# Four of the eight batches of x1 are read back during the expert tiles, and VectorE adds one and a half of them

## The chip, the core and the metric

The kernel runs on one core of a Trainium2 chip. The metric is the time on the device, in microseconds (us), of one execution; lower is better. Times in a trace are counted from the start of its span.

## The reference

The input x has 8 batches of 512 tokens with 256 features. Two blocks follow each other, each of the form x + layernorm(block(layernorm(x))):

```python
x = x + layernorm(s4d(layernorm(x)))      # x1: state-space convolution over 512 tokens (by FFT), skip, layernorm
x = x + layernorm(moe(layernorm(x)))      # 8 experts, each token goes to its best 2
# moe: z = layernorm(x); w = softmax weights of the top 2 experts, scaled to sum 1
#      x + sum over experts of w[e] * (gelu(z @ W1[e] + b1[e]) @ W2[e] + b2[e])
```

What matters here is the last line: the output is x1 plus the normalised result of the second block. The kernel calls the first block's result x1 and the second block's result, summed over a token's two experts, y.

## The kernel before, in words

All of it is one program in which each engine runs its own list of instructions, ordered by hand, and waits on semaphores. SyncE (`sp`) issues all plain DMA transfers, on one queue, in the order of its list. GpSimd (`pool`) issues the indirect ones.

First comes the s4d block, one batch at a time. Each batch of x1 (128 partitions x 4 x 256 numbers, 512 KB) is stored to a DRAM buffer `x1_dram`, and the normalised rows are scattered by expert into `z_rows`. Then come the tiles: 71 (`TILES`) tiles of 128 rows, each of one expert. The first 14 (`FIRST`) are taken while the last batch is still being routed; from tile 14 on the remaining tiles run through the experts in order, so that the first expert is through at the latest with tile 14 + 32 - 1. For a tile SyncE reads its rows (`load_z`, two buffers), PE transposes them, does the first layer (`first_layer`, L1487), transposes the hidden rows and does the second layer (`second_layer`, L1511, which counts up `l2_mm`). ScalarE weighs the result and GpSimd scatters it, adding, into `y_rows`. `load_z(t)` waits until tile t-2 has been transposed, and `release(t)` lets GpSimd's scatters go on. The weights of all eight experts stay in SBUF for the whole time (`ws`, 16 KB of each partition for one expert, from offset 0). In tiles 20, 21 and 22 SyncE also reads the batches 7, 6 and 5 of x1 back into `x1m` (L446).

When the last scatter has landed, the tail begins. The eight batches are taken from the last to the first; n counts them (n = 0 is batch 7). SyncE reads y of each into `yr`, over the place of the weights (L459). Ahead of n = 2 it reads batch 4 of x1 (L456), ahead of n = 6 the batches 0 to 3 in one transfer (L458). For each n VectorE takes mean and variance (`spread_of`, L1224 and L1227), ScalarE the root (`root`, L706), VectorE the factors (`scale`, L1235 to L1237), ScalarE writes the normalised batch into `acc` in four instructions (`close`, L711; `m_fin` counts finished batches, and the last one in two halves), GpSimd adds x1 in place (`add`, L1331, counts `m_out`), and SyncE stores it (L463). Of the last batch GpSimd adds the first half and VectorE the second (L1248, `m_last`). VectorE's list runs two batches ahead: `scale(n)` comes before `spread_of(n + 2)`, and a wait in the one holds the next.

Of the kernel before, what the change touches and what calls it, by code (L numbers as in the profile page):

```python
# [17 lines left out]
F32 = mybir.dt.float32  # L18
# [7 lines left out]
P = 128  # L26
B, T, H, N = 8, 512, 256, 64
# [11 lines left out]
HEAD = 5  # L39
FIRST = -(-(HEAD * T - (E - 1) * (P - 1)) // P)  # L40
ROWS = E * REGION
ROUND = 12582912.0
TURN = 6.283185
W = H + 3
TRASH = B * T
KB = 1024
# [20 lines left out]
def program(nc, x, fwd_tab, inv_tab, lag_tab, swap_in, phase_in, ident_in, upper_in, tile_tab, lar, aim, cre, cim,  # L67
            ldt, d_skip, ln_w, ln_b, ffn_g, ffn_b, r_w, r_b, w1, b1, w2, b2, out, dbg=None):
    sems = {}

    def sem(name):
        if name not in sems:
            sems[name] = nc.alloc_semaphore(name)
        return sems[name]

    def at(name, shape, dt, off):
        return nc.alloc_sbuf_tensor_at(name, shape, dt, offset=BASE + off)
# [88 lines left out]
    x1m = at("x1m", [P, B, 4, H], F32, 112 * KB + 64)  # L166
# [23 lines left out]
    cmp_t = at("cmp_t", [P, TILES + 1 - FIRST, E], F32, o0 + 64)  # L190
    tf = at("tf", [P, 3, TILES + 1], F32, o0 + 2560)
    iot = at("iot", [P, 3, TILES + 1], F32, o0 + 12544)
    yr = at("yr", [P, B, 4, H], F32, 0)
    acc = at("acc", [P, B, 4, H], F32, 64 * KB)
    psum = nc.alloc_psum_tensor("psum", [P, 8 * 512], F32)

# [41 lines left out]

    z_rows = nc.dram_tensor("z_rows", [ROWS, W], F32, kind="Internal").ap()
    y_rows = nc.dram_tensor("y_rows", [B * T + 2 * P, H], F32, kind="Internal").ap()  # L240
    x1_dram = nc.dram_tensor("x1_dram", [P, B, 4, H], F32, kind="Internal").ap()
# [13 lines left out]
    def gate(eng):  # L255

        eng.sem_inc(sem("gate"), 1)
# [30 lines left out]
    def buf(b):  # L288

        return (0, 1, 2, 3, 0, 1, 4, 5)[b]  # L290

    def sent(b):

        return 128 * (1 + (b in (4, 5)))
# [19 lines left out]
    def slot_of(b):  # L314

        return (0, 1, 2, 3, 7, 6, 5, 4)[b]

    with nc.Block() as block:

        @block.sync  # L320
        def _(sp):
# [61 lines left out]
            def load_z(t):  # L383

                if t in (0, FIRST):
                    sp.wait_ge(sem("tab_ready"), 1 + (t == FIRST))
                row = sp.value_load(tab[0:1, 0, t:t + 1], min_val=0, max_val=ROWS - P)
                if t >= 2:
# [11 lines left out]
            def pad(e):  # L400

                behind = sp.value_load(padi[0:1, e:e + 1], min_val=0, max_val=ROWS - P)
                sp.dma_start(z_rows[bass.ds(behind, P), :], zpad[:, :]).then_inc(sem("pads"), 16)
# [36 lines left out]
            for t in range(FIRST, TILES):  # L440
                load_z(t)
                release(t - 6)
                if 20 <= t < 23:

                    b = B - 1 - (t - 20)
                    sp.dma_start(x1m[:, slot_of(b)], x1_dram[:, b]).then_inc(sem("x1_in"), 16)  # L446
            for t in range(TILES - 6, TILES):
                release(t)

# [3 lines left out]
            sp.wait_ge(sem("y_out1"), 16 * (TILES // 2))  # L453
            for n in range(B):
                if n == 2:
                    sp.dma_start(x1m[:, slot_of(4)], x1_dram[:, 4]).then_inc(sem("x1_in"), 16)  # L456
                if n == 6:
                    sp.dma_start(x1m[:, 0:4], x1_dram[:, 0:4]).then_inc(sem("x1_in"), 16)  # L458
                sp.dma_start(yr[:, n], y_tok[:, B - 1 - n]).then_inc(sem(f"y_in{n}"), 16)  # L459
            for n in range(B):  # L460
                sp.wait_ge(sem("m_out"), n + 1)
                ks = slice(0, 2 if n == B - 1 else 4)
                sp.dma_start(out[:, B - 1 - n, ks], acc[:, n, ks]).then_inc(sem("stored"), 16)  # L463
            sp.wait_ge(sem("m_last"), 1)
            sp.dma_start(out[:, 0, 2:4], acc[:, B - 1, 2:4]).then_inc(sem("stored"), 16)
            sp.wait_ge(sem("stored"), 16 * (B + 1))

        @block.scalar
        def _(act):
# [254 lines left out]
        def _(dve):  # L724
            seq = Seq(dve, sem("dve_seq"))
            V = nc.vector
# [48 lines left out]
            V.memset(one_half[:, :], 0.5)  # L775
            V.memset(rnd[:, :], ROUND).then_inc(sem("one"), 1)
            seq.inc(V.memset(carry_b[:, :], 0.0))
# [22 lines left out]
            do(V.tensor_scalar(ang[:, 3], theta, T / 2.0, None, ALU.mult))  # L800
            do(V.tensor_scalar(sm[:, 10:14], ang[:, :, :, :], ROUND, ROUND, ALU.add, ALU.subtract))
            V.tensor_tensor(ang[:, :, :, :], ang[:, :, :, :], sm[:, 10:14], ALU.subtract).then_inc(sem("k_ang"), 1)
# [439 lines left out]
            for n in range(B):  # L1242
                scale(n)
                if n + 2 < B:
                    spread_of(n + 2)
            dve.wait_ge(sem("m_fin"), B + 1)
            dve.wait_ge(sem("x1_in"), 80)
            V.tensor_tensor(acc[:, B - 1, 2:4], acc[:, B - 1, 2:4], x1m[:, 0, 2:4], ALU.add).then_inc(sem("m_last"), 1)  # L1248

        @block.gpsimd  # L1250
        def _(pool):
            G = nc.gpsimd
            def combine(row, u):
                n, par = row.b * 2 + u, row.par
                pool.wait_ge(sem("mult_done"), n + 1)
                ks = slice(2 * u, 2 * u + 2)
                G.tensor_tensor(yf[par][:, 0, ks], yf[par][:, 0, ks], tmp[u][:, 0],  # L1257
                                ALU.subtract).then_inc(sem("yf_ready"), 1)
                G.tensor_tensor(yf[par][:, 1, ks], yf[par][:, 1, ks], tmp[u][:, 1],  # L1259
                                ALU.add).then_inc(sem("yf_ready"), 1)  # L1260

            def fold(b):

                pool.wait_ge(sem("xn_ready"), b + 1)
                G.tensor_tensor(pm[b][:, 0], xn[b % 3][:, 0:2], xn[b % 3][:, 2:4], ALU.add).then_inc(sem("pm_ready"), 1)  # L1265
                G.tensor_tensor(pm[b][:, 1], xn[b % 3][:, 0:2], xn[b % 3][:, 2:4], ALU.subtract).then_inc(sem("pm_ready"), 1)

            def scatter(row, lo, hi):

                pool.wait_ge(sem("pos_ready"), row.b + 1)  # L1270
                for i in range(lo, hi):
                    pool.indirect_dma_start(z_rows, bass.IndirectOffsetOnAxis(ap=pos[row.par][:, i // 4, i % 4:i % 4 + 1], axis=0),  # L1272
                                            zn[buf(row.b)][:, i % 4], None).then_inc(sem(f"scattered{buf(row.b)}"), 16)

            def step(n):
                nxt, cur, tail, last_tail = (Row(n, k) for k in (1, 0, -2, -LAG))

                last = Row(n, -LAG - 1)
                if cur.live and cur.b:
                    if cur.b > 1:  # L1280
                        pool.wait_ge(sem("x1_mean"), cur.b - 1)
                    combine(cur, 1)
                if last.live and n <= B:
                    scatter(last, 3, 8)
                if nxt.live:
                    if nxt.b > 1:
                        pool.wait_ge(sem("o_ready"), nxt.b - 1)
                    combine(nxt, 0)
                    if nxt.b == 0:
                        combine(nxt, 1)  # L1290
                if last_tail.live and n < B:
                    scatter(last_tail, 0, 3)
                elif n == B:
                    scatter(last_tail, 0, 8)
                    scatter(tail, 0, 8)
                for b in FOLDS.get(n, ()):
                    fold(b)

            for b in range(4):
                fold(b)  # L1300
            for n in range(-1, B + 1):
                step(n)


            def scatter_y(t):

                q = t % 2
                if t:
                    pool.wait_ge(sem("released"), t)
                    gate(pool)  # L1310
                if t >= 2:
                    pool.wait_ge(sem(f"y_out{q}"), (t - q) * 8)
                    gate(pool)
                pool.wait_ge(sem("yw_ready"), t + 1)
                gate(pool)
                pool.indirect_dma_start(y_rows, bass.IndirectOffsetOnAxis(ap=dst[t % 8][:, 0:1], axis=0),  # L1316
                                        yw[t % 6][:, :], None, compute_op=ALU.add).then_inc(sem(f"y_out{q}"), 16)

            for b in range(2, B):
                pool.wait_ge(sem(f"zn_stored{buf(b)}"), sent(b) // 8)  # L1320
            pool.wait_ge(sem("trash_set"), 32)
            for t in range(TILES):
                if t == EARLY:
                    scatter(Row(B - 1, 0), 0, 8)
                scatter_y(t)

            def add(n, ks):
                pool.wait_ge(sem("m_fin"), n + 1)
                if n in (0, 3):
                    pool.wait_ge(sem("x1_in"), 80 if n else 48)  # L1330
                G.tensor_tensor(acc[:, n, ks], acc[:, n, ks], x1m[:, slot_of(B - 1 - n), ks], ALU.add).then_inc(sem("m_out"), 1)  # L1331

            for n in range(B):
                add(n, slice(0, 2 if n == B - 1 else 4))

        @block.tensor
        def _(pe):
# [300 lines left out]
```

## Time and profile before

| | |
|---|---|
| median of 3 runs | 563.23 us (562.65 to 569.51) |
| profiled execution, its own time | 566.21 us |
| its span | 564.4 us |
| mean granted clock of TensorE | 0.913 |
| busy: PE, VectorE, ScalarE, GpSimd | 81%, 79%, 67%, 47% of the span |

The trace is of one execution, whose own time is the span with 1.8 us around it. The tail from the first read of y (530.94 us) to the end of the span is 33.5 us, in which PE does nothing.

### The profile page before, as it was taken

How to read it: one execution, taken by the hardware profiler on the slowest of the kernel's cores; microseconds unless marked ns; L12 is line 12 of the kernel's file. 1: busy time of each engine (PE TensorE's matmuls, PEld its weight loads, DVE VectorE, ACT ScalarE, POOL GpSimd, SP SyncE). 2: the span in 40 equal slices, each digit the busy share in tenths (PEclk: the TensorE clock that was granted, in tenths of full speed). 3: DMA queues.
4: the chain of work that ended last, by engine and by line, in shares of the span. 5: the costliest groups of instructions: out<-in, count | busy, mean ns of one | idle time of the engine just before them, and what ended most of it. 6: DMA issues, size and time to landing. Idle time of an engine off the chain costs nothing.

```text
span 564.4 us, 11667 instructions
## 1 busy us (share of the span) xinstructions
PE 455.0 (81%) x2730; PEld 393.6 (70%) x2730; DVE 443.1 (79%) x1492; ACT 377.3 (67%) x928; POOL 267.3 (47%) x195
## 2 busy tenths in 40 slices
PE   0296899978999988468868999999999999999100
PEld 0136888857988876247757888999999999998100
DVE  6999785999898987765766878877888878887282
ACT  6991864455666656767634777777777777776184
POOL 0000349544566877365175344445444444445365
PEclk9997989988999996687986999999999999999655
DMA  6303730042224466496145458444555545444696
GB/s 166 135 1 121 285 117 1 0 130 77 104 94 153 152 213 208 137 326 219 30 133 94 80 93 189 77 77 77 78 79 82 80 82 77 77 72 54 145 400 273
DMA packets 47615, 70.35 MB, mean 125 GB/s; under 512 B 7616, under 2 KB 37184, under 8 KB 47040
## 3 DMA queue, kind: packets, MB, share of 16 engines
q1 hardware_dynamic: 34256, 51.82, 27.6%
q0 software_dynamic: 13296, 17.80, 19.1%
q8 instruction: 26, 0.43, 0.3%
q14 instruction: 37, 0.30, 0.2%
HBM read 37.90 MB, written 31.70 MB: 123 GB/s over the span
## 4 chain that ended last, share of the span: by engine, by line
PE 51%; DVE 24%; ACT 10%; issue 5%; DMA 4%; POOL 2%; another core or an unknown queue 1%; SPq 1%; DVEq 1%; POOLq 0%; ACTq 0%
PE psum L1487 16%; PE psum L1511 15%; PE psum L1497 5%; PE psum L1407 4%; DVE ws L934 2%; PE psum L1471 2%; DMA yr<-y_rows 2%; DVE st L739 2%; PE psum L1378 2%; PE psum L1365 2%; PE psum L1427 2%; ACT xn L492 1%; DMA y_rows<-yw,dst 1%; ACT dump L652 1%; ACT ws L589 1%
## 5 line engine op out<-in xcount | busy, mean ns | idle before, releaser
L1316 POOL DMA_INDIRECT y_rows<-yw,dst x71 | 113.1, 1593 | 142.1 <-SPq L398 76.6
L1487 PE MATMUL psum<-ws,z_hl 128*128 x426 | 120.7, 420 | 9.3 <-DVE ws L934 6.4
L1511 PE MATMUL psum<-ws,h_hl 128*128 x852 | 118.3, 289 | 0.6 <-DVE h_hl L1100 0.6
L1511 PEld LDWEIGHTS psum<-ws,h_hl 128*128 128x128 f32 x852 | 105.8, 192 | 0.8 <-issue 0.8
L1487 PEld LDWEIGHTS psum<-ws,z_hl 128*128 128x128 f32 x426 | 77.3, 195 | 24.4 <-issue 11.2
L1272 POOL DMA_INDIRECT z_rows<-zn,pos x64 | 70.2, 1097 | 28.8 <-issue 17.1
L634 ACT ACTIVATE hg<-hb 128x512 f32<-128x512 f32 x71 | 44.9, 633 | 33.8 <-DVE hb L1094 32.0
L597 ACT ACTIVATE z_f<-psum,gb 128x128 f32<-128x128 f32 x142 | 57.2, 453 | 10.5 <-issue 4.5
L1407 PE MATMUL psum<-yf,it 128*128 128x256 f32 x256 | 62.0, 400 | 2.6 <-DVE r L1121 2.6
L1378 PE MATMUL psum<-pm,ft 128*128 128x256 f32 x256 | 59.9, 390 | 0.4 <-DVE tmp L920 0.2
L627 ACT CAST h_hl<-psum 128x512 fp32r<-128x512 f32 x71 | 41.5, 585 | 25.7 <-PE psum L1497 21.4
L1407 PEld LDWEIGHTS psum<-yf,it 128*128 128x128 f32 x256 | 50.9, 202 | 10.6 <-POOL yf L1259 3.2
L1081 DVE CAST z_hl<-z_f 128x256 fp32r<-128x256 f32 x71 | 21.0, 295 | 43.6 <-PE psum L1487 35.1
L1378 PEld LDWEIGHTS psum<-pm,ft 128*128 128x128 f32 x256 | 48.9, 195 | 7.7 <-issue 1.1
L1094 DVE TENSOR_TENSOR hb<-psum,b1r 128x512 f32<-128x512 f32 x71 | 48.5, 684 | 5.5 <-remote 3.1
L1100 DVE TENSOR_TENSOR h_hl<-psum,h_hl 128x512 fp32r<-128x512 f32 x71 | 48.3, 680 | 2.3 <-ACT h_hl L627 2.0
L1497 PE MATMUL psum<-ident,hg 128*128 128x128 f32 x284 | 43.5, 276 | 1.6 <-ACT hg L634 1.4
L1497 PEld LDWEIGHTS psum<-ident,hg 128*128 128x128 f32 x284 | 35.9, 142 | 12.3 <-ACT hg L634 2.5
L1257 POOL TENSOR_TENSOR yf<-yf,tmp 128x512 f32<-128x512 f32 x16 | 24.4, 1523 | 39.4 <-DVE o L1147 29.7
L1265 POOL TENSOR_TENSOR pm<-xn 128x512 f32<-128x512 f32 x8 | 10.2, 1280 | 68.8 <-ACT xn L492 68.8
L607 ACT ACTIVATE yw<-y_sb,wt 128x256 f32<-128x256 f32 x71 | 35.7, 503 | 4.5 <-DVE y_sb L1111 3.2
L1083 DVE TENSOR_TENSOR z_hl<-z_f,z_hl 128x256 fp32r<-128x256 f32 x71 | 30.2, 426 | 2.4
(222 smaller groups left out, 843.3 us busy)
## 6 DMA issues: line engine op xcount, KB each, us to landing
z_in<-z_rows SPq DMA_DIRECT2D x71, 129.5 KB
w_raw<-in_dram SPq DMA_DIRECT2D x16, 512.0 KB, 5.9
xs<-in_dram SPq DMA_DIRECT2D x8, 512.0 KB, 5.4
x_dram<-xs SPq DMA_DIRECT2D x8, 512.0 KB
y_rows<-zn SPq DMA_DIRECT2D x8, 512.0 KB, 3.3
yr<-y_rows SPq DMA_DIRECT2D x8, 512.0 KB, 7.2
out_dram<-acc SPq DMA_DIRECT2D x7, 512.0 KB, 5.1
b1r<-in_dram SPq DMA_DIRECT2D x8, 256.0 KB
```

Source lines behind the costliest of these rows:

```text
L597: last = nc.scalar.activation(z_f[:, k], ps_z[:, k], ACT.Identity, bias=gb[:, 1, k:k + 1], scale=gb[:, 0, k:k + 1])
L627: nc.scalar.copy(h_hl[t % 2][:, 0], ps_t).then_inc(sem("h_high"), 1)
L634: nc.scalar.activation(hg[t % 2][:, :], hb[:, :], ACT.Gelu).then_inc(sem("hg_ready"), 1)
L1094: V.tensor_tensor(hb[:, :], ps_h[t % 2], b1r[:, bass.ds(e, 1)].rearrange("p a f -> p (a f)"), ALU.add).then_inc(sem("hb_ready"), 1)
L1100: V.tensor_tensor(h_hl[t % 2][:, 1], ps_t, h_hl[t % 2][:, 0].bitcast(F32), ALU.subtract).then_inc(sem("h_split"), 1)
L1272: pool.indirect_dma_start(z_rows, bass.IndirectOffsetOnAxis(ap=pos[row.par][:, i // 4, i % 4:i % 4 + 1], axis=0), zn[buf(row.b)][:, i % 4] ...
L1316: pool.indirect_dma_start(y_rows, bass.IndirectOffsetOnAxis(ap=dst[t % 8][:, 0:1], axis=0), yw[t % 6][:, :], None, compute_op=ALU.add).the ...
L1378: last = TE.matmul(fw[u][c][:, k], ft[:, c, t, kt * P:(kt + 1) * P], pm[row.b][:, c, t], start=t == 0, stop=t == 1)
L1407: last = TE.matmul(iv[c][:, j * H:(j + 1) * H], it[:, c, k, j * P:(j + 1) * P], yf[row.par][:, c, k], start=k == 0, stop=k == KT - 1)
L1487: last = TE.matmul(ps_h[q], z_hl[q][:, a, k], w_at(e, c, k * F, F), start=n == 0, stop=n == 5)
L1497: last = TE.transpose(ps_t[:, k], hg[t % 2][:, k * P:(k + 1) * P], ident[:, :])
L1511: last = TE.matmul(ps_y[q], h_hl[q][:, a, k], w_at(e, c, 1024 + k * H, H), start=n == 0, stop=n == 11)
```

## The change

Four batches of x1 (0 to 3) get a buffer of their own, `x1a`, at offset 0, the place of the first expert's weights; `yr` moves 16 KB further on. SyncE reads them one by one after the reads of z for the tiles 56, 58, 60 and 62, behind a wait for 46 finished second layers. The 2 MB read ahead of n = 6 goes. Batch 4 keeps its place ahead of n = 2 and has its own semaphore. GpSimd's first add now waits for all seven batches that are read during the tiles. GpSimd adds the batches n = 0 to 5 and the first half of n = 6; VectorE adds the second half of n = 6 and both halves of n = 7. The stores of the last two batches are four halves, in the order in which the list expects them.

```diff
+LATE = (56, 58, 60, 62)
...
-    yr = at("yr", [P, B, 4, H], F32, 0)
+    yr = at("yr", [P, B, 4, H], F32, 16 * KB)
+    x1a = at("x1a", [P, 4, 4, H], F32, 0)
...
+    def x1_of(b):
+
+        return x1a[:, b] if b < 4 else x1m[:, slot_of(b)]
...
+                if t in LATE:
+
+                    sp.wait_ge(sem("l2_mm"), FIRST + B * T // P)
+                    b = 3 - LATE.index(t)
+                    sp.dma_start(x1a[:, b], x1_dram[:, b]).then_inc(sem("x1_in"), 16)
...
                 if n == 2:
-                    sp.dma_start(x1m[:, slot_of(4)], x1_dram[:, 4]).then_inc(sem("x1_in"), 16)
-                if n == 6:
-                    sp.dma_start(x1m[:, 0:4], x1_dram[:, 0:4]).then_inc(sem("x1_in"), 16)
+                    sp.dma_start(x1m[:, slot_of(4)], x1_dram[:, 4]).then_inc(sem("x1_four"), 16)
                 sp.dma_start(yr[:, n], y_tok[:, B - 1 - n]).then_inc(sem(f"y_in{n}"), 16)
-            for n in range(B):
+
+            def store(n, lo, hi):
+
+                sp.dma_start(out[:, B - 1 - n, lo:hi], acc[:, n, lo:hi]).then_inc(sem("stored"), 16)
+
+            for n in range(B - 2):
                 sp.wait_ge(sem("m_out"), n + 1)
-                ks = slice(0, 2 if n == B - 1 else 4)
-                sp.dma_start(out[:, B - 1 - n, ks], acc[:, n, ks]).then_inc(sem("stored"), 16)
+                store(n, 0, 4)
+            sp.wait_ge(sem("m_half"), 1)
+            store(B - 2, 2, 4)
             sp.wait_ge(sem("m_last"), 1)
-            sp.dma_start(out[:, 0, 2:4], acc[:, B - 1, 2:4]).then_inc(sem("stored"), 16)
-            sp.wait_ge(sem("stored"), 16 * (B + 1))
+            store(B - 1, 0, 2)
+            sp.wait_ge(sem("m_out"), B - 1)
+            store(B - 2, 0, 2)
+            sp.wait_ge(sem("m_last"), 2)
+            store(B - 1, 2, 4)
+            sp.wait_ge(sem("stored"), 16 * (B + 2))
...
-            dve.wait_ge(sem("m_fin"), B + 1)
-            dve.wait_ge(sem("x1_in"), 80)
-            V.tensor_tensor(acc[:, B - 1, 2:4], acc[:, B - 1, 2:4], x1m[:, 0, 2:4], ALU.add).then_inc(sem("m_last"), 1)
+            dve.wait_ge(sem("x1_in"), 112)
+            dve.wait_ge(sem("m_fin"), B - 1)
+            V.tensor_tensor(acc[:, B - 2, 2:4], acc[:, B - 2, 2:4], x1_of(1)[:, 2:4], ALU.add).then_inc(sem("m_half"), 1)
+            for u in range(2):
+                dve.wait_ge(sem("m_fin"), B + u)
+                ks = slice(2 * u, 2 * u + 2)
+                V.tensor_tensor(acc[:, B - 1, ks], acc[:, B - 1, ks], x1_of(0)[:, ks], ALU.add).then_inc(sem("m_last"), 1)
...
             def add(n, ks):
                 pool.wait_ge(sem("m_fin"), n + 1)
-                if n in (0, 3):
-                    pool.wait_ge(sem("x1_in"), 80 if n else 48)
-                G.tensor_tensor(acc[:, n, ks], acc[:, n, ks], x1m[:, slot_of(B - 1 - n), ks], ALU.add).then_inc(sem("m_out"), 1)
-
-            for n in range(B):
-                add(n, slice(0, 2 if n == B - 1 else 4))
+                if n == 0:
+                    pool.wait_ge(sem("x1_in"), 112)
+                if n == 3:
+                    pool.wait_ge(sem("x1_four"), 16)
+                G.tensor_tensor(acc[:, n, ks], acc[:, n, ks], x1_of(B - 1 - n)[:, ks], ALU.add).then_inc(sem("m_out"), 1)
+
+
+            for n in range(B - 1):
+                add(n, slice(0, 2 if n == B - 2 else 4))
```

## Rows read from the trace of the kernel before

**Rows 1.** The head of the page.
```profile
span 564.4 us, 11667 instructions
```

**Rows 2.** The chain of waits in the tail: start us, us, what.
```profile
534.88 13.45 DMA yr<-y_rows
```

**Rows 3.** Stretches: us, busy and instructions of each engine, clock, DMA share, GB/s.
```profile
535.00:541.00 6.00, 0.00 (x0) 0.00 (x0) 5.76 (x31) 3.00 (x8) 0.31 (x1) 0.50 1.02 416
```

**Rows 4.** VectorE's timeline: start us, us, what, idle before and releaser.
```profile
547.15 0.16 DVE L1237 TENSOR_TENSOR rm<-xb,psum 128x4 f32<-128x4 f32 x1
548.35 1.40 DVE L1224 BATCH_NORM_STATS2 st<-yr 128x6 f32<-128x256 f32 x4 [1.04 <-DMA yr<-y_rows]
...
556.95 1.07 DVE L1248 TENSOR_TENSOR acc<-acc,x1m 128x512 f32<-128x512 f32 x1 [3.45 <-ACT acc L711]
```

**Rows 5.** ScalarE's timeline in the tail.
```profile
538.53 2.07 ACT L711 ACTIVATE acc<-yr,rm 128x256 f32<-128x256 f32 x4 [0.20 <-DVE rm L1237]
...
547.35 2.08 ACT L711 ACTIVATE acc<-yr,rm 128x256 f32<-128x256 f32 x4
...
550.67 2.07 ACT L711 ACTIVATE acc<-yr,rm 128x256 f32<-128x256 f32 x4 [0.20 <-DVE rm L1237]
...
552.88 4.04 ACT L711 ACTIVATE acc<-yr,rm 128x256 f32<-128x256 f32 x8
```

**Rows 6.** GpSimd's timeline in short windows; a row with x2 holds two instructions.
```profile
540.69 2.35 POOL L1331 TENSOR_TENSOR acc<-acc,x1m 128x1024 f32<-128x1024 f32 x1 [11.98 <-ACT acc L711]
...
547.59 4.67 POOL L1331 TENSOR_TENSOR acc<-acc,x1m 128x1024 f32<-128x1024 f32 x2
...
552.82 2.35 POOL L1331 TENSOR_TENSOR acc<-acc,x1m 128x1024 f32<-128x1024 f32 x1 [0.56 <-ACT acc L711]
...
555.12 4.02 POOL L1331 TENSOR_TENSOR acc<-acc,x1m 128x1024 f32<-128x1024 f32 x2
...
557.43 1.71 POOL L1331 TENSOR_TENSOR acc<-acc,x1m 128x512 f32<-128x512 f32 x1
```

**Rows 7.** SyncE's timeline, the last three stores.
```profile
557.50 0.33 SPq L463 DMA_DIRECT2D out_dram<-acc  x1
559.17 0.33 SPq L463 DMA_DIRECT2D out_dram<-acc  x1
559.54 0.43 SPq L465 DMA_DIRECT2D out_dram<-acc  x1
```

**Rows 8.** SyncE's waits from 526 us on: us in total, times, longest.
```profile
SPq L318 <- DMA out_dram<-acc: 2.4, 1, 2.4
SPq L318 <- PEq L318: 1.8, 1, 1.8
```

**Rows 9.** The timeline of tiles 20 to 22, SyncE's reads of x1.
```profile
338.04 0.33 SPq L446 DMA_DIRECT2D x1m<-x_dram  x1
...
340.26 0.33 SPq L446 DMA_DIRECT2D x1m<-x_dram  x1
...
342.95 0.33 SPq L446 DMA_DIRECT2D x1m<-x_dram  x1
```

**Rows 10.** The chain of waits in the same tiles.
```profile
337.39 1.40 PE psum L1487 x6
...
340.84 1.41 PE psum L1487 x6
...
344.30 0.45 issue
344.74 1.66 PE psum L1487 x6
...
348.45 1.41 PE psum L1487 x6
```

**Rows 11.** Stretches with the third of those reads, and of quiet tiles (columns as in group 3).
```profile
341.00:344.50 3.50, 3.30 (x24) 2.78 (x22) 2.85 (x10) 2.75 (x8) 1.56 (x1) 1.00 1.04 253
...
440.00:460.00 20.00, 20.00 (x140) 18.18 (x140) 16.50 (x53) 15.83 (x41) 10.01 (x7) 1.00 0.51 81
```

## The prediction

> **What bounds the kernel now.** I read the page first, then the chain of waits, then each engine's timeline of the last 35 us, and last the stretch of the tiles in which the kernel already reads x1. The span is 564.4 us [rows 1]. The change touches two stretches: the tiles, where the order of the work is PE's, and the tail after the last tile. Nothing before the reads of tile 56 changes, and y's new place, 16 KB further on, moves no instruction.
>
> In the tail the chain of waits shows one long piece: the seventh read of y, issued at 534.88, lands 13.45 us later, at 548.33 [rows 2]. It stands behind the read of four batches of x1 (2 MB). In that stretch the DMA engines are full, at 416 GB/s [rows 3]. VectorE has finished its small work on the batch before at 547.31 and sits idle for 1.04 us until that read lands [rows 4]. ScalarE's scaling of the sixth batch inherits it: the first five follow each other at (547.35 - 538.53) / 4 = 2.20 us, the sixth comes 3.32 us after the fifth [rows 5], so 1.12 us late. GpSimd, which adds x1, is the slower engine (2.35 us a batch; 2.30 from start to start): it keeps busy through five batches and could start the sixth at 547.59 + 2 x 2.30 = 552.2, but idles 0.56 us and starts it at 552.82 [rows 6]. From then on GpSimd sets the end: two whole batches and half of the last, finished at 557.43 + 1.71 = 559.14. SyncE then issues two stores, at 559.17 and 559.54 [rows 7]; the last one is waited for 2.4 us and 1.8 us of closing waits follow [rows 8]. From the start of the last store to the end of the span: 564.4 - 559.54 = 4.86 us.
>
> **The change, part by part.**
>
> Reads leave the tail. Four batches are 2.1 MB; at 416 GB/s that is 5.0 us less in front of the seventh and eighth y. The seventh then lands near 548.33 - 5.0 = 543.3, 4 us before VectorE wants it at 547.31. The 1.04 us idle goes. ScalarE's sixth batch starts at 547.35 + 2.20 = 549.55 and ends at 551.6. The seventh and eighth shift by the same 1.12 us: the seventh ends at 552.88 + 2.07 - 1.12 = 553.83, the eighth's first half at 554.82, its second at 556.92 - 1.12 = 555.80. What is late next is GpSimd: its sixth add starts when the fifth is done, 552.2 instead of 552.82. This step alone is worth 0.6 us, not 1.1.
>
> Half of batch seven and the first half of batch eight go from GpSimd to VectorE. GpSimd then ends its sixth add at 552.2 + 2.35 = 554.55 and has half a batch left; VectorE has three halves, ready at 553.83, 554.82 and 555.80. What they cost beside each other is read from the one place where both add. VectorE's half ran from 556.95 to 558.02 [rows 4]. GpSimd's whole add had begun at 555.12 and ended at 555.12 + 2.35 = 557.47, and its half ran from 557.43 to 559.14 [rows 6]. So VectorE's ended 0.55 us after GpSimd's whole add, and GpSimd's half 1.12 us after VectorE's; half of 2.35 is 1.18. That looks like taking turns: each instruction spends its overlap waiting and then needs 0.55 (VectorE) or 1.12 (GpSimd). I count in turn: from 554.55, three halves of 0.55 and one of 1.12 make 2.8, so everything is added at 557.3 to 557.4, whichever engine goes first. Before, the same count after GpSimd's sixth add (555.17) was 2.30 + 0.55 + 1.12 = 3.97. The gain of this step is 1.2 us.
>
> If instead the two only slow each other, the durations 1.07 and 1.71 stand for themselves: VectorE 553.85 + 3 x 1.07 = 557.06, GpSimd 554.5 + 1.71 = 556.2, done at 557.1. With no interference at all VectorE's last half would end at 555.80 + 0.55 = 556.4 and GpSimd's at 555.7. These are the good end; the bad end is the turns, with a start that slips.
> The Trainium skill (SBUF — State Buffer, Who interferes with whom) says that a VectorE instruction with both inputs in SBUF contends with a GpSimd instruction that reads SBUF, and that one of them blocks for the other's whole instruction. By that rule the end of the adds is the 557.4 of the turns, and without it the 557.1 of the plain durations; it speaks against moving the adds to VectorE, and the two durations above fit it.
>
> Stores. The last two are reordered into four halves. If VectorE ends last, SyncE has already issued the third and the last starts at about 557.45; if GpSimd ends last, two stores follow each other as before (0.37 us apart) and the last starts at about 557.8. I take 557.6, against 559.54: 1.9 us earlier. In the 2 us before it 1 MB of stores is under way, the same as before (one whole batch and two halves), so I keep the 4.86 us behind it. Were the stores closer together than that, 0.26 MB at 416 GB/s would add 0.6 us.
>
> Four reads enter the tiles. SyncE issues each in 0.33 us behind a tile's read of z [rows 9]. The new wait in front of them asks for 46 finished second layers. Behind it in SyncE's queue stand the next reads of z (PE waits for them) and the releases of GpSimd's scatters. It costs nothing: the read of z for tile 56, just ahead, has waited for the transposes of tile 54, which PE issues after the second layer of tile 50. The reads' own cost has one precedent, the three reads at tiles 20 to 22, one a tile. PE's chain shows one disturbance there: 0.45 us of "issue" and a first layer of 1.66 instead of 1.41 us [rows 10], 0.70 us in all, behind the third read, where the DMA share stood at 1.04 against 0.51 in a quiet stretch [rows 11]. The first two reads cost nothing. The new reads come every second tile, 6.9 us apart. One read of 0.52 MB takes 1.26 us of all engines, so the share over two tiles rises to about 0.51 + 1.26 / 6.9 = 0.69, and no pile like that of the third read should form. Bounds: 0 and 4 x 0.70 / 3 = 0.93 us; between them no row decides, and I take the middle, 0.45. GpSimd's first add waits for all seven reads in the tiles; the last is issued near 342.95 + 40 x 3.45 = 481, almost 60 us ahead of that add. The fifth batch keeps its place in the tail, third in the queue, and the fourth add that waits for it comes at 547.59.
>
> **Sum.** -0.6 (stall) - 1.2 (adds) - 0.1 (stores) + 0.45 (tiles) = -1.4 us. The profiled execution took 566.21 us (564.4 of it the span) and would take 564.8. That run stands 3.0 us above the median of the runs, 563.23, so I forecast 561.8. Nothing under 2% (11 us) can be told from no change here, and this change cannot reach it.
>
> **The rivals.**
> The adds run side by side: the last store starts between 556.5 and 557.15, 2.4 to 3.0 us early; less 0.45, the time is 560.7 to 561.3. For it: a good part of VectorE's 1.07 us might be sharing. Against it: the ends 0.55 and 1.12 us after each other.
> Slower: each late read stalls PE once. The place is the first layer after a read, the price the 0.70 us of the third read, so 2.8 us, and 563.23 - 1.9 + 2.8 = 564.1. It decides as soon as one read costs over 0.48 us. For it: z of the next tile is queued behind half a megabyte on the same queue. Against it: two of the three reads known cost nothing, and they came at twice the rate.
> The reads go and the end stays with the stores: four half stores and the whole one pile up and the last lands 0.6 us later, or the adds slip; half the gain is lost, 562.7 or so.
> A larger effect, a lower clock or long stalls of PE in the last tiles, has no row for it.
>
> **How the numbers follow.** The forecast has 0.50 (its own range 561.0 to 562.6), side by side 0.20, the lost gain 0.15, the stalling reads 0.12, something larger 0.03. The runs shown spread from 562.65 upward, so half a microsecond goes on either side: from 560.0, below the best of side by side, to 564.6, above the stalling reads. Faster by over 2%: 0.01; within: 0.97; slower: 0.02.
>
> **What would show it.** VectorE's seventh statistics follow at once, with no wait on a read of y. GpSimd has six whole adds in one row without idle time, and a half. The three VectorE adds and that half do not finish before 557.3 if they take turns, counted from the first add at 540.69. Tiles 56 to 63 keep the 3.45 us each of the tiles before (340.84 - 337.39 [rows 10]) but for one stall. Wrong it would be if PE shows a gap behind each read, if a VectorE half took 0.55 us beside a GpSimd add, or if the last store were waited for clearly over 2.4 us.

## The result and the profile after

The change made the kernel faster, by a little more than I forecast: 560.53 us median against 563.4 us, a difference of 2.9 us. The ratio of the means is 0.9936 with a 95% interval of 0.9910 to 0.9962, that is 3.6 us (2.1 to 5.1). I had forecast 561.8, a gain of 1.4 us, and had written that nothing under 2% can be told from no change here; the interval does tell it. The time lies inside the range and the direction is right; the size of the gain is not.

The head of the page of the kernel after, against [rows 1]; the profiled execution took 560.84 us:

```profile
span 558.8 us, 11672 instructions
```

The first read of y starts anywhere from 526.5 to 530.9 us in the traces of this study, so I count the tail from its own marks. From the first read of y to the end of the span it took 564.4 - 530.94 = 33.46 us before and 558.8 - 528.11 = 30.69 us after: 2.77 us less.

SyncE's timeline after, the reads of the tail and the last store, against [rows 7] (start us, us, what):

```profile
528.11 0.81 SPq L468 DMA_DIRECT2D yr<-y_rows  x2
528.96 0.43 SPq L467 DMA_DIRECT2D x1m<-x_dram  x1
529.43 2.96 SPq L468 DMA_DIRECT2D yr<-y_rows  x6
...
554.95 0.46 SPq L472 DMA_DIRECT2D out_dram<-acc  x1
```

VectorE's timeline after, against [rows 4]: the seventh statistics, at 544.51, follow the factors before them with no wait on a read. The only wait on y left is that for the first one.

```profile
531.78 1.41 DVE L1243 BATCH_NORM_STATS2 st<-yr 128x6 f32<-128x256 f32 x4 [9.24 <-DMA yr<-y_rows]
...
544.43 0.16 DVE L1256 TENSOR_TENSOR rm<-xb,psum 128x4 f32<-128x4 f32 x1
544.51 1.41 DVE L1243 BATCH_NORM_STATS2 st<-yr 128x6 f32<-128x256 f32 x4
...
551.21 1.19 DVE L1267 TENSOR_TENSOR acc<-acc,x1a 128x512 f32<-128x512 f32 x1 [1.55 <-ACT acc L730]
552.32 1.75 DVE L1271 TENSOR_TENSOR acc<-acc,x1a 128x512 f32<-128x512 f32 x1
...
553.99 0.68 DVE L1271 TENSOR_TENSOR acc<-acc,x1a 128x512 f32<-128x512 f32 x1
```

ScalarE's timeline after, against [rows 5]: the sixth batch follows the fifth 2.21 us later, where it was 3.32.

```profile
544.62 2.08 ACT L730 ACTIVATE acc<-yr,rm 128x256 f32<-128x256 f32 x4
...
546.83 2.08 ACT L730 ACTIVATE acc<-yr,rm 128x256 f32<-128x256 f32 x4
...
549.03 4.04 ACT L730 ACTIVATE acc<-yr,rm 128x256 f32<-128x256 f32 x8
```

GpSimd's timeline after, in short windows as in [rows 6]: the first row has the first four adds, then come the sixth and the half behind it. No row after the first has idle time in front of it.

```profile
537.96 9.28 POOL L1356 TENSOR_TENSOR acc<-acc,x1m 128x1024 f32<-128x1024 f32 x4 [12.20 <-ACT acc L730]
...
549.47 2.38 POOL L1356 TENSOR_TENSOR acc<-acc,x1a 128x1024 f32<-128x1024 f32 x1
...
551.77 1.75 POOL L1356 TENSOR_TENSOR acc<-acc,x1a 128x512 f32<-128x512 f32 x1
```

SyncE's waits in the tail after, against [rows 8]: the last store lands 2.1 us after its issue and 1.0 us of closing waits follow, where it was 2.4 and 1.8.

```profile
SPq L324 <- DMA out_dram<-acc: 2.1, 1, 2.1
...
SPq L324 <- PEq L324: 1.0, 1, 1.0
```

Here is the surprise. From the first GpSimd add, the last add of all ends at 554.67 - 537.96 = 16.71 us, as forecast (557.35 - 540.69 = 16.7), and the last store starts at 16.99 instead of 18.85, 1.86 us earlier, as forecast too (1.9). But behind it only 558.8 - 554.95 = 3.85 us follow, not the 4.86 that I kept. That is 1.0 us of gain that I had not counted, more than half of the 1.4 us that I forecast.

The chain of waits in the late tiles has one gap in PE, against [rows 10]: 0.15 us of issue and 0.25 us in the first layer, 0.40 us in all. I had put 0.45 there.

```profile
482.92 1.41 PE psum L1513 x6
...
486.38 0.15 issue
486.53 1.66 PE psum L1513 x6
...
490.24 1.41 PE psum L1513 x6
```

### The profile page after: what moved, and what is told of

It is laid out like the page before. It is cut to its first block, busy times and chain, and to the rows that moved or that the text cites. A ratio compares the mean times of both kernels' runs of the same rounds, so it can differ in the third digit from the quotient of the medians.

```text
span 558.8 us, 11672 instructions
## 1 busy us (share of the span) xinstructions
PE 450.2 (81%) x2730; PEld 388.9 (70%) x2730; DVE 445.0 (80%) x1494; ACT 376.2 (67%) x928; POOL 263.4 (47%) x194
## 4 chain that ended last, share of the span: by engine, by line
PE 48%; DVE 26%; ACT 14%; issue 6%; DMA 2%; POOL 1%; DVEq 1%; SPq 1%; another core or an unknown queue 0%; ACTq 0%; POOLq 0%
PE psum L1513 17%; PE psum L1537 15%; PE psum L1523 5%; PE psum L1497 3%; DVE ws L953 3%; ACT acc L730 2%; PE psum L1433 2%; DVE st L758 2%; PE psum L1391 2%; ACT dump L671 2%; DVE o L1166 1%; ACT ws L608 1%; PE psum L1404 1%; PE psum L1453 1%; DVE vq L885 1%
## 5 line engine op out<-in xcount | busy, mean ns | idle before, releaser
L1339 POOL DMA_INDIRECT y_rows<-yw,dst x71 | 111.2, 1566 | 144.4 <-SPq L404 84.1
L1404 PE MATMUL psum<-pm,ft 128*128 128x256 f32 x256 | 58.2, 382 | 0.4 <-DVE tmp L939 0.4
L1497 PE MATMUL psum<-ident,z_in 128*128 128x128 f32 x142 | 27.5, 276 | 7.2 <-issue 4.1
```

The lines of the kernel that those rows point to most:

```text
L1404: last = TE.matmul(fw[u][c][:, k], ft[:, c, t, kt * P:(kt + 1) * P], pm[row.b][:, c, t], start=t == 0, stop=t == 1)
L1497: last = TE.transpose(ps_z[:, k], z_in[q][:, k * P:(k + 1) * P], ident[:, :])
```

## The experiments

Two questions: why fewer microseconds follow the last store, and whether the terms of the sum are each of the size I gave them. The theories on the first were three: A, the closing varies from one execution to the next; B, it belongs to the kernel and hangs on the last store and the order of the stores; and C, which came out of the first four runs, it hangs on GpSimd.

**Both kernels again**, unchanged.

> The kernel before, unchanged, to see what one execution differs from the next. Ratio 1.00 by every theory. Theory A (the closing after the last store varies from one execution to the next, and the first trace of before had a long one): from the start of the last store to the end of the span comes out other than 4.86 us, at 3.8 to 4.9. Theory B (the closing belongs to the kernel: its last two stores follow 0.37 us apart): 4.86 us again, to 0.2 us. Both: from the first GpSimd add to the last store 18.85 us again, to 0.1 us, and at most one stall of PE after tile 23.

Ratio 1.0009 (0.9986 to 1.0032). The last store starts 18.86 us after the first add, and 4.83 us follow. The two traces of this kernel agree, so A has nothing left for it.

> The kernel after, unchanged. Theory A: the closing after the last store varies and may come out up to 4.9 us; theory B: 3.85 us again, to 0.2 us. Both: from the first GpSimd add to the last store 17.0 us. The tiles: if the late reads stall PE, one or more gaps of 0.4 to 0.7 us between tiles 56 and 66 again; if the one gap seen was chance, none or somewhere else. Ratio 0.993 to 0.996.

Ratio 0.9931 (0.9904 to 0.9959). The last store starts 556.22 - 539.25 = 16.97 us after the first add, and 3.88 us follow. PE has one gap in the late tiles, 0.66 us, this time right behind the third read.

**The reads alone.** The adds and stores of the kernel before, put into the kernel after:

```diff
...
-            dve.wait_ge(sem("m_fin"), B - 1)
-            V.tensor_tensor(acc[:, B - 2, 2:4], acc[:, B - 2, 2:4], x1_of(1)[:, 2:4], ALU.add).then_inc(sem("m_half"), 1)
...
+            dve.wait_ge(sem("m_fin"), B + 1)
+            V.tensor_tensor(acc[:, B - 1, 2:4], acc[:, B - 1, 2:4], x1_of(0)[:, 2:4], ALU.add).then_inc(sem("m_last"), 1)
...
-            for n in range(B - 1):
-                add(n, slice(0, 2 if n == B - 2 else 4))
+            for n in range(B):
+                add(n, slice(0, 2 if n == B - 1 else 4))
```

> The late reads and the tail without the 2 MB read, but the adds and stores of the kernel before. By my sum: GpSimd adds without idle, the last store 18.85 - 0.63 = 18.2 us after the first add. Theory A: closing between 3.8 and 4.9 us; theory B: 4.8 us, as before. Tiles 0 to 0.9 us longer. Ratio 0.999 to 1.000. A rival, that the reads alone bring most of the gain, would give 17.0 to 17.5 us and a ratio of 0.995.

Ratio 0.9990 (0.9963 to 1.0017). The 1.04 us wait for the seventh y is gone, but in this execution the second and third y came a little late, VectorE waited 0.30 and 0.27 us, and GpSimd idled 0.21 us. The last store starts 18.50 us after the first add, where 18.2 was expected, and 4.89 us follow. The gain is small, as expected, and not the bulk of the whole.

**The adds alone.** The reads of the kernel before (2 MB ahead of the seventh y), the adds and stores of the one after:

```diff
-LATE = (56, 58, 60, 62)
...
+                if n == 6:
+                    sp.dma_start(x1m[:, 0:4], x1_dram[:, 0:4]).then_inc(sem("x1_in"), 16)
...
```

> The reads of the kernel before, the adds and stores of the one after. By turns, with GpSimd's stall of 0.63 us kept and ScalarE's last batches 1.12 us late: 17.2 to 17.3 us from the first add to the last add, last store 17.3 us after the first add. Theory A: closing between 3.8 and 4.9 us; theory B: 3.85 us, as in the kernel after. No gap in PE beyond what the kernel before has. Ratio 0.995 to 0.998.

Ratio 0.9981 (0.9957 to 1.0004). The last add ends 17.35 us after the first one, where turns gave 17.2 to 17.3. The tail is 560.9 - 529.64 = 31.26 us, 2.2 us shorter than before; the runs show 0.0019 of 563.9, 1.1 us (-0.2 to 2.4). The last store starts at 557.11, 17.62 us after the first add, 0.3 us later than expected, and 3.8 us follow: the closing that B had forecast. So these four runs leave B standing.

Laid side by side, though, the four runs and the first two traces had one constant that was in neither theory: the span ends 5.21 to 5.30 us after the end of GpSimd's last add, whatever VectorE and the stores do. The next run was made to decide between B and this.

**GpSimd last of all**, in one execution.

```diff
                 add(n, slice(0, 2 if n == B - 2 else 4))
+            pool.wait_ge(sem("m_last"), 2)
+            G.memset(flag[:, :], 0.0)
```

> The kernel after, and behind its last add GpSimd waits for VectorE's last add and writes 128 numbers that nobody reads. Times from the first GpSimd add (kernel after: GpSimd's last add ends at 15.56, the last store starts at 16.99, the span ends at 20.84). Theory C (the span ends about 5.25 us after GpSimd's last instruction, which was so in all six traces, 5.21 to 5.30): GpSimd's last instruction ends at 16.85, the span at 22.1. Theory B (the end hangs on the last store, and the closing behind it on the order of the stores): 20.8, unchanged, since no store waits for the new instruction.

The span ends 559.6 - 537.49 = 22.11 us after the first add, 1.27 us later than in the kernel after, though no store waits for the new instruction and the last store starts where it did (16.98). GpSimd's timeline in that kernel:

```profile
537.49 9.27 POOL L1356 TENSOR_TENSOR acc<-acc,x1m 128x1024 f32<-128x1024 f32 x4 [11.99 <-ACT acc L730]
...
554.26 0.10 POOL L1362 MEMSET flag<- 128x1 f32 x1 [1.21 <-DVE acc L1271]
```

SyncE's waits there: the last store lands after 2.1 us as before, and the closing wait behind it grows from 1.0 to 2.3 us. The wait is put down to PE's queue, which had nothing to do for 30 us; the engine that was late is GpSimd.

```profile
SPq L324 <- PEq L324: 2.3, 1, 2.3
SPq L324 <- DMA out_dram<-acc: 2.1, 1, 2.1
```

**No contest for SBUF.** ScalarE writes the halves that VectorE adds into PSUM:

```diff
...
+    fin = {(B - 2, 1): bank(6), (B - 1, 0): bank(7), (B - 1, 1): bank(3)}
...
-                    last = nc.scalar.activation(acc[:, n, k], yr[:, n, k], ACT.Identity,
+                    last = nc.scalar.activation(closed(n, k // 2)[:, k % 2], yr[:, n, k], ACT.Identity,
...
-                V.tensor_tensor(acc[:, B - 1, ks], acc[:, B - 1, ks], x1_of(0)[:, ks], ALU.add).then_inc(sem("m_last"), 1)
+                V.tensor_tensor(acc[:, B - 1, ks], closed(B - 1, u), x1_of(0)[:, ks], ALU.add).then_inc(sem("m_last"), 1)
```

> The kernel after, but ScalarE puts the halves that VectorE adds into PSUM, so that VectorE's three adds have one input in SBUF. By turns (an add with two SBUF inputs and a GpSimd add take turns): no waiting any more, VectorE's halves take about 0.68 us each, the last ends at 15.8 us after the first GpSimd add instead of 16.71, GpSimd's half takes 1.2 us instead of 1.75 and ends at 15.0. If the two slow each other in another way, 1.07 to 1.2 us a half again and 16.7. End of the span: by theory C 15.0 + 5.25 = 20.2; by theory B 15.9 + 3.85 = 19.7. Ratio to before 0.992.

Ratio 0.9969 (0.9948 to 0.9989). VectorE's timeline in this kernel:

```profile
550.49 0.69 DVE L1274 TENSOR_TENSOR acc<-psum,x1a 128x512 f32<-128x512 f32 x1 [1.52 <-ACT psum L737]
551.41 0.69 DVE L1278 TENSOR_TENSOR acc<-psum,x1a 128x512 f32<-128x512 f32 x1 [0.22 <-ACT psum L737]
552.39 0.69 DVE L1278 TENSOR_TENSOR acc<-psum,x1a 128x512 f32<-128x512 f32 x1 [0.29 <-ACT psum L737]
```

And GpSimd's, in a short window, its half batch:

```profile
551.11 1.27 POOL L1363 TENSOR_TENSOR acc<-acc,x1a 128x512 f32<-128x512 f32 x1
```

VectorE's first two halves take 0.69 us each beside GpSimd's adds, where they took 1.19 and 1.75; GpSimd's half takes 1.27 where it took 1.75. VectorE's last add ends at 553.08 - 537.28 = 15.80, as turns had it. The span ends at 20.32, 5.22 us after GpSimd's last add, as C had it (20.2), and not at 19.7 as B had it. The ratio is a miss: 0.992 was expected, and the runs show no gain over the kernel after (0.9931 to 0.9955 in three comparisons), though in its trace the span ends 0.5 us sooner after the first add. Why, I do not know; the intervals overlap.

**Six adds on GpSimd, two batches on VectorE**, both inputs in SBUF. The last two batches are then stored in three parts, the seventh whole and the eighth in halves:

```diff
...
-            V.tensor_tensor(acc[:, B - 2, 2:4], acc[:, B - 2, 2:4], x1_of(1)[:, 2:4], ALU.add).then_inc(sem("m_half"), 1)
+            V.tensor_tensor(acc[:, B - 2], acc[:, B - 2], x1_of(1), ALU.add).then_inc(sem("m_half"), 1)
...
-            for n in range(B - 1):
-                add(n, slice(0, 2 if n == B - 2 else 4))
+            for n in range(B - 2):
+                add(n, slice(0, 4))
```

> The kernel after, but GpSimd adds only six whole batches and VectorE all of the last two (both inputs in SBUF). GpSimd's last add ends 13.9 us after its first. VectorE: a whole batch from 13.9 to 15.0, the halves to 15.7 and 16.3; last store at 16.35. Theory C: 13.9 + 5.25 = 19.1, unless the last store with its 2.1 to 2.5 us of landing ends later, then 19.2 to 19.5. Theory B: 16.35 + 3.85 = 20.2. Ratio to before 0.990 to 0.992.

Ratio 0.9916 (0.9899 to 0.9933). The span ends 19.72 us after the first add, 1.1 us sooner than in the kernel after. GpSimd's last add ends at 550.65, 5.85 us before the end, more than the 5.2 to 5.3 of the others: it is no longer what the end waits for. SyncE's waits there: the store's landing comes last, and almost no closing wait is left.

```profile
SPq L324 <- DMA out_dram<-acc: 2.5, 1, 2.5
SPq L324 <- PEq L324: 0.2, 1, 0.2
```

**Both together**, six adds on GpSimd and two batches added from PSUM (the two edits above, with all four halves of the last two batches in PSUM).

> Both together: GpSimd adds six whole batches, VectorE two, from PSUM. VectorE's last add ends 15.8 us after GpSimd's first, the last store starts at 15.9 and lands by 18.5. Theory C: 13.9 + 5.25 = 19.1. Theory B: 15.9 + 3.85 = 19.7. Ratio to before 0.990, to the kernel after 0.997.

Ratio 0.9931 (0.9918 to 0.9945). The last add ends at 15.80 as expected, but the last store's issue is done at 16.76, no earlier than with six adds alone (16.83), its landing takes 2.7 us, and the span ends at 19.84, where C had 19.1 and B 19.7. GpSimd is out of the way here, so the two theories are not told apart by it. The 0.36 us of faster adds are lost between SyncE's issue and the landing; which of the two costs how much I did not separate. The ratio, expected at 0.990, is a miss too.

**The two best beside each other.**

> Six whole adds on GpSimd, VectorE the last two batches, beside the kernel after on the same chip. The trace of its first run ended 19.7 us after GpSimd's first add, 1.1 us sooner than the kernel after, and there the last store's landing ended last (2.5 us, then 0.2 us), not GpSimd (5.85 us before the end). Expected again: 19.6 to 19.8; ratio to before 0.990 to 0.993, about 0.002 under the kernel after in this call.

> The kernel after, beside the one above. Span end 20.8 us after GpSimd's first add and 5.2 to 5.3 us after GpSimd's last. If the gain in the runs is what the traces show (2.8 us in the tail, 0 to 0.7 us given back in the tiles), the ratio to before is 0.995 to 0.996; if the runs hold another gain that the traces do not show, 0.993 as twice before.

Six adds: ratio 0.9932 (0.9907 to 0.9957), end 19.90 us after the first add (6.01 after GpSimd's last). Kernel after: 0.9955 (0.9935 to 0.9975), end 20.80 (5.27 after GpSimd's last), one gap in PE of 0.44 us. The six-add version is clearly faster than the kernel before; over the kernel after it is 0.9 to 1.1 us ahead in the tails of the traces, while the intervals of the runs overlap.

**The late reads one a tile.**

```diff
-LATE = (56, 58, 60, 62)
+LATE = (56, 57, 58, 59)
```

> The kernel after with its four late reads after the tiles 56, 57, 58 and 59, one a tile as in tiles 20 to 22. If the stall of PE comes of reads piling up, one or two stalls of 0.3 to 0.7 us within four tiles of the third read. If it is chance (with reads two tiles apart four traces of seven had one stall, three had none), none or one, and anywhere from tile 56 on. Tail as in the kernel after: end 20.8 us after GpSimd's first add.

In this one execution the reads pile up, and further than expected: three tiles in a row come late. PE's timeline around the third read (467.26) and the fourth (469.29) shows one transpose that waits for its rows of z, and two first layers that start late. Three tiles take 477.91 - 466.05 = 11.86 us, 1.5 us more than 3 x 3.45. Only 0.19 us of it is put down to the landing of z; the late first layers stand as "issue", and what held them is not shown.

```profile
466.05 0.38 PE L1497 MATMUL psum<-ident,z_in 128*128 128x128 f32 x2
...
469.84 0.44 PE L1497 MATMUL psum<-ident,z_in 128*128 128x128 f32 x2 [0.19 <-DMA z_in<-z_rows]
470.69 1.66 PE L1513 MATMUL psum<-ws,z_hl 128*128 x6 [0.41 <-issue]
474.02 0.38 PE L1497 MATMUL psum<-ident,z_in 128*128 128x128 f32 x2
474.60 1.67 PE L1513 MATMUL psum<-ws,z_hl 128*128 x6 [0.19 <-issue]
477.91 0.38 PE L1497 MATMUL psum<-ident,z_in 128*128 128x128 f32 x2
```

The stretch from 470 to 474 us in that kernel, against [rows 11] (columns as there):

```profile
470.00:474.00 4.00, 3.59 (x24) 3.05 (x24) 2.69 (x8) 2.60 (x7) 0.00 (x0) 1.00 1.06 297
```

All marks in one table, in us from the start of GpSimd's first add, worked out from the timelines and spans ("issued" is the end of SyncE's issue; the spans are read to 0.1 us):

| kernel | GpSimd's last instruction ends | VectorE's last add ends | last store issued | span ends | end less GpSimd's last |
|---|---|---|---|---|---|
| before | 18.45 | 17.33 | 19.28 | 23.71 | 5.26 |
| before, again | 18.45 | 17.34 | 19.29 | 23.69 | 5.24 |
| reads alone | 18.10 | 16.97 | 18.93 | 23.39 | 5.29 |
| adds alone | 16.20 | 17.35 | 18.07 | 21.41 | 5.21 |
| after | 15.56 | 16.71 | 17.44 | 20.84 | 5.28 |
| after, again | 15.55 | 16.70 | 17.42 | 20.85 | 5.30 |
| after, third | 15.53 | 16.69 | 17.42 | 20.80 | 5.27 |
| GpSimd last of all | 16.87 | 16.71 | 17.44 | 22.11 | 5.24 |
| halves from PSUM | 15.10 | 15.80 | 16.90 | 20.32 | 5.22 |
| late reads one a tile | 15.56 | 16.71 | 17.44 | 20.79 | 5.23 |
| six adds | 13.87 | 16.16 | 16.83 | 19.72 | 5.85 |
| six adds, again | 13.89 | 16.18 | 16.85 | 19.90 | 6.01 |
| six adds, from PSUM | 13.86 | 15.80 | 16.76 | 19.84 | 5.98 |

In the first ten rows, those up to the late reads one a tile, the last column is 5.21 to 5.30, while the last store moves by 2.4 us. Only where GpSimd is done early does the landing of the stores take over.

The traces also show what the end waits for. The line that opens the block of engine programs (L324) holds each engine's closing instructions, among them a DRAIN (count, least/median/most ns, first and last start in us). In the kernel after:

```profile
L324 POOLq DRAIN  x1: 7406/7406/7406, 551.1 to 551.1; - x1
L324 DVEq DRAIN  x1: 1605/1605/1605, 553.1 to 553.1; - x1
L324 SPq DRAIN  x1: 7/7/7, 557.7 to 557.7; - x1
```

With GpSimd last of all:

```profile
L324 POOLq DRAIN  x1: 5132/5132/5132, 554.2 to 554.2; - x1
```

With six adds:

```profile
L324 POOLq DRAIN  x1: 7931/7931/7931, 547.8 to 547.8; - x1
...
L324 SPq DRAIN  x1: 7/7/7, 556.3 to 556.3; - x1
```

GpSimd's DRAIN ends at 558.5, 559.3 and 555.7, each time 5.0 us after its last instruction; VectorE's ends within 0.1 us of its last add. In the first two kernels GpSimd's DRAIN is the last of all, and the span ends 0.2 to 0.3 us behind it. With six adds SyncE's is the last, at 556.3.

## Why the prediction was wrong in its size

*The stall goes* (-0.6): right. VectorE's wait for the seventh y is gone, ScalarE's batches follow each other at 2.2 us to the end, GpSimd adds seven times without idle time.

*The adds, taken in turn* (-1.2): right, to 0.1 us. In the trace after, GpSimd's sixth add ends at 549.47 + 2.38 = 551.85, VectorE's half at 552.40, 0.55 later, GpSimd's half at 553.52, 1.12 later, VectorE's next half at 554.07, 0.55 later; the last half, alone, takes 0.68 and ends at 554.67. These distances are the 0.55 and 1.12 of the prediction, three times over. That the second input in SBUF is what makes the engines take turns is shown by the kernel that takes one input from PSUM: 0.69 us a half beside the same GpSimd adds. The rival of adds side by side falls.

*The stores* (-0.1): right; the last starts 1.86 us earlier, forecast 1.9.

*"So I keep the 4.86 us behind it"*: this is the step that failed. I took the end of the span for a fixed distance from the last store. It is a fixed distance, 5.2 to 5.3 us, from the end of GpSimd's last instruction, as long as the stores have landed by then, and the run with one idle instruction more on GpSimd shows it: the end moves with it by 1.27 us, while the stores stay where they were. GpSimd's last add moved from 18.45 to 15.56 us after its first, 2.9 us, and so did the end, 23.71 to 20.84. The sum should have counted GpSimd's work alone: 0.6 us of stall, and 2.3 us for the whole batch that becomes a half and the half that goes. VectorE's last adds lay beside GpSimd's closing; they cost only the 0.5 us by which GpSimd's half waits for its turn (1.75 us here, 1.27 beside adds from PSUM). The row that could have told me was on my list: 1.8 us of closing waits after the last store had landed [rows 8]. Something else was still late there, and I carried it along as overhead.

*The late reads* (+0.45): right in size, for the kernel as it is. From the transposes of tile 55 to those of tile 70 the three traces without late reads take 51.74 to 51.92 us, the nine with reads two tiles apart 51.74 to 52.51, on average 0.3 us more. Five of the nine have a gap of 0.3 to 0.7 us at the third read, one a gap of 0.4 behind the fourth, three at most 0.2 in all. The one trace with reads one a tile takes 53.27. The row that I priced from was one draw: the same three reads at tiles 20 to 22, one a tile in every kernel here, cost from nothing to 1.1 us in the thirteen traces. The rival of one stall at each read falls. Its mechanism, z queued behind half a megabyte, is shown for 0.19 us of the 1.5 that the reads one a tile cost; the rest is open.

With GpSimd's end put in, the steps give -2.9 + 0.45, about -2.4 us, and the traces 2.77 us in the tail less 0.40 in the tiles, also 2.4. The runs gave 3.6 (2.1 to 5.1), then 0.9931 and 0.9955 of 563.9 and 564.4 us, 3.9 (2.3 to 5.4) and 2.5 us (1.4 to 3.7). All three intervals hold 2.4, the first two only near their lower end. So the traces account for 2.4 us, and a further microsecond may be there that they do not explain. It would have to arise ahead of the tail: PE's transposes of tile 14 start at 316.3 to 319.8 us in the three traces without late reads and at 314.2 to 317.4 in the ten with them. The two ranges overlap and no run was made on it, so this stays open.

## What to carry to other kernels

A kernel ends when the last of all its engines has closed, not when its last store has landed: take the time from each engine's last instruction to the end of the span, and see which of these distances stays the same when work moves. If a wait remains after the last landing, the end belongs to some engine, and work should leave that engine first; the name that the profile gives for such a wait need not be the late one. Where VectorE adds two inputs from SBUF beside GpSimd's adds, count the instructions one after the other, or give VectorE one input in PSUM.

## What was not expected of the hardware

GpSimd needs 5.2 to 5.3 us from its last instruction to the end of the span (ten traces), against about 3.0 us from the end of the last store's issue where the store decides (556.5 - 553.61 = 2.9, 557.4 - 554.35 = 3.05). For 5.0 us of it the traces have GpSimd in its closing DRAIN; what that waits for they don't show. Four transfers of 512 KB cost the tiles 0 to 0.8 us when two tiles apart (nine traces) and 1.5 us when one apart (one trace, with the DMA share at 1.06).
